# Layer-norm powers moved from GpSimd's power operation to a logarithm, an exponential and one Newton step, with a rewritten order table

## The reference

```python
def _ln_t(v, eps=1e-05):
    m = jnp.mean(v, axis=-1, keepdims=True)
    s = jnp.var(v, axis=-1, keepdims=True)
    return (v - m) / jnp.sqrt(s + eps)
...
t = t + _L1_attn_ref(_ln_t(t), ...)
t = t + _L1_ffn_ref(_ln_t(t), ...)
```

## Time and profile before

| | before |
|---|---|
| median of 3 runs | 2406.02 us (2404.33 to 2406.26) |
| the profiled execution, time | 2404.97 us |
| its span, first to last instruction | 2403.2 us |
| busy PE, DVE, POOL, ACT | 2183.1, 2062.3, 1839.2, 1516.3 us |

### The profile page before, as it was taken

The page is one execution under the profiler, slowest core; times in us unless marked ns, Lnnn a source line. Parts: engine busy times, 40 slices in busy tenths (PEclk is TensorE's granted clock), DMA queues, the critical chain, the costliest instruction groups (busy, mean ns, idle before and its releaser), DMA issues.

```text
span 2403.2 us, 44296 instructions
## 1 busy us (share of the span) xinstructions
PE 2183.1 (91%) x15620; PEld 1098.5 (46%) x15620; DVE 2062.3 (86%) x2694; ACT 1516.3 (63%) x2757; POOL 1839.2 (77%) x1553
## 2 busy tenths in 40 slices
PE   5379999999999999999999999999999999999972
PEld 5224444444444444444444444444444444444441
DVE  5257899999999999999999999999999999999853
ACT  0157767667666666666667666676676766766630
POOL 0314688888888888888888888888888888888786
PEclk8589999999999999999999999999999999999985
DMA  9442323323343243344432343344322333332111
GB/s 235 121 55 39 62 50 59 68 55 65 72 71 65 55 55 68 57 60 72 72 68 59 51 65 65 52 72 72 72 61 52 58 68 54 66 65 61 28 28 34
DMA packets 485705, 156.59 MB, mean 65 GB/s; under 512 B 438688, under 2 KB 472336, under 8 KB 485360
## 3 DMA queue, kind: packets, MB, share of 16 engines
q1 hardware_dynamic: 485488, 153.75, 35.1%
HBM read 95.41 MB, written 51.38 MB: 61 GB/s over the span
## 4 chain that ended last, share of the span: by engine, by line
POOL 35%; PE 25%; DVE 17%; ACT 10%; issue 10%; DMA 3%; SPq 0%; POOLq 0%; ACTq 0%; DVEq 0%
POOL rstd L819 11%; POOL qbuf L838 7%; DVE qbuf L1018 6%; POOL prod L877 5%; ACT ebuf L727 4%; PE ps L619 4%; POOL xn L825 4%; PE ps L645 3%; POOL prod L880 3%; PE ps L593 3%; PE ps L610 3%; PE ps L636 2%; ACT ebuf L722 2%; POOL xcs L833 2%; PE ps L658 2%
## 5 line engine op out<-in xcount | busy, mean ns | idle before, releaser
L727 ACT ACTIVATE ebuf<-ps,small 128x896 f32<-128x896 f32 x448 | 450.3, 1005 | 163.7 <-PE ps L610 150.0
L838 POOL TENSOR_TENSOR qbuf<-spread_r,qbuf 128x896 f32<-128x896 f32 x224 | 469.4, 2096 | 94.4 <-ACT spread_r L759 94.4
L1018 DVE SCALAR_TENSOR_TENSOR qbuf<-ps,ebuf 128x896 f32<-128x896 f32 x448 | 484.9, 1082 | 58.9 <-ACT ebuf L727 58.3
L1012 DVE SCALAR_TENSOR_TENSOR kbuf<-ps,ebuf 128x1024 f32<-128x1024 f32 (+1 forms) x416 | 487.6, 1172 | 48.2 <-ACT ebuf L722 44.7
L722 ACT ACTIVATE ebuf<-ps,small 128x1024 f32<-128x1024 f32 (+1 forms) x416 | 448.0, 1077 | 116.0 <-DVE kbuf L1012 68.2
L593 PE MATMUL ps<-kbuf,xcs 128*64 128x512 f32 (+1 forms) x1600 | 440.4, 611 | 7.7 <-DVE kbuf L1012 4.0
L819 POOL TENSOR_TENSOR rstd<-varr,power 112x28 f32<-112x28 f32 x64 | 307.2, 4800 | 164.9 <-DVE varr L996 164.8
L645 PE MATMUL ps<-qbuf,gmat 128*64 128x224 f32 x3584 | 386.2, 357 | 1.6 <-DVE pbuf L1041 1.0
L645 PEld LDWEIGHTS ps<-qbuf,gmat 128*64 128x64 f32 x3584 | 248.5, 136 | 154.6 <-issue 51.3
L1097 DVE TENSOR_TENSOR prod<-ps,gate 112x1024 f32<-112x1024 f32 x224 | 273.0, 1220 | 52.2 <-PE ps L670 37.1
L877 POOL TENSOR_TENSOR prod<-prod 112x512 f32<-112x512 f32 x224 | 285.6, 1275 | 20.9 <-DVE prod L1097 20.3
(11 more groups left out here) (132 smaller groups left out, 3129.0 us busy)
## 6 DMA issues: line engine op xcount, KB each, us to landing
z<-zd SPq DMA_DIRECT2D x256, 196.0 KB, 3.8
zd<-zhl SPq DMA_DIRECT2D x64, 392.0 KB, 2.4
qbuf<-in_x SPq DMA_DIRECT2D x16, 784.0 KB, 9.5
xt<-in_x SPq DMA_DIRECT2D x256, 49.0 KB
xd<-xn SPq DMA_DIRECT2D x128, 98.0 KB, 2.9
out<-ffn SPq DMA_DIRECT2D x256, 49.0 KB
xkt<-xd SPq DMA_DIRECT2D x32, 384.0 KB, 6.6
shifted<-nat SPq DMA_DIRECT2D x128, 52.6 KB, 5.3
```

The lines of the kernel that those rows point to most:

```text
L727: act.activation(ebuf[:, 1, 0:2 * G * PT].rearrange("p (a b) -> p a b", a=2), o[:, :, 0:G * PT], ACT.Exp, bias=minus_one).then_inc(qexp_ma ...
L838: nc.gpsimd.tensor_tensor(qbuf[:, 2:4, n, :], spread_r[:, :, :], qbuf[:, 2:4, n, :], ALU.mult)\
L1012: v.scalar_tensor_tensor(kbuf[0:w, m.at(KS, n) % 2, 0:DH * c].rearrange("p (a b) -> p a b", a=c), o[0:w, 0:c, :], 1.0, ebuf[0:w, 0, 0:DH * ...
L1018: v.scalar_tensor_tensor(qbuf[:, k0:k0 + 2, j, :], o[:, :, 0:G * PT], 1.0, ebuf[:, 1, 0:2 * G * PT].rearrange("p (a b) -> p a b", a=2), AL ...
```

## The change

The power of the two layer norms is taken apart. Before, POOL raised `varr` to -0.5 in one instruction. Now ACT takes a logarithm of the scaled variance, an exponential of -0.5 times that (a seed for the reciprocal root) and a square, as new steps LV1 and LV2 in ACT's order, each instruction waiting for the one ahead of it; POOL then makes one Newton step of three small instructions, again each waiting for the last. ACT's table of functions is named ahead of the loop, before ACT's first wait. Two other powers, ahead of the loop, stay.

```diff
+SEED = 2.0 ** -20
...
         @block.scalar
         def _(act):
+            nc.scalar.preload_act_table_set("natural_log_exp_and_others")
             act.wait_ge(dve_pre, 6)
...
+                elif kind in ("LV1", "LV2"):
+                    ln = kind == "LV2"
+                    act.wait_ge(var_made[ln], m.at(1, 1))
+                    act.activation(lnv[ln][:, :], varr[ln][:, :], ACT.Ln, scale=SEED * SEED).then_inc(seed_step[ln], 1)
+                    act.wait_ge(seed_step[ln], m.at(2, 1))
+                    act.activation(seed[ln][:, :], lnv[ln][:, :], ACT.Exp, scale=-0.5).then_inc(seed_step[ln], 1)
+                    act.wait_ge(seed_step[ln], m.at(2, 2))
+                    act.activation(newton[ln][:, :], seed[ln][:, :], ACT.Square, scale=SEED).then_inc(seed_made[ln], 1)
...
                 if kind in ("PN1", "PN2"):
                     ln = kind == "PN2"
-                    pool.wait_ge(var_made[ln], m.at(1, 1))
-                    nc.gpsimd.tensor_tensor(rstd[ln][:, :], varr[ln][:, :], power[0:PT, 0:SLOTS], ALU.pow)\
+                    pool.wait_ge(seed_made[ln], m.at(1, 1))
+                    nc.gpsimd.tensor_tensor(newton[ln][:, :], newton[ln][:, :], varr[ln][:, :], ALU.mult)\
+                        .then_inc(newton_step[ln], 1)
+                    pool.wait_ge(newton_step[ln], m.at(2, 1))
+                    nc.gpsimd.tensor_scalar(newton[ln][:, :], newton[ln][:, :], -0.5 * SEED, 1.5 * SEED, ALU.mult, ALU.add)\
+                        .then_inc(newton_step[ln], 1)
+                    pool.wait_ge(newton_step[ln], m.at(2, 2))
+                    nc.gpsimd.tensor_tensor(rstd[ln][:, :], seed[ln][:, :], newton[ln][:, :], ALU.mult)\
                         .then_inc(rstd_made[ln], 1)
```

All numbers of ORDER are new. Two lines of it, PE's F:

```diff
-        "F": [34.99, 35.66, 36.49, 37.53, 38.78, 40.49, 41.98],
+        "F": [37.013, 37.217, 38.036, 38.813, 40.476, 42.242, 43.704],
```

More of the change, by code:

```diff
@@ L122 @@
     "tensor": {
[17 rows of a table removed]
[17 rows of a table added]
     },
     "vector": {
[16 rows of a table removed]
[16 rows of a table added]
     },
     "scalar": {
[L160 to L176, removed]
+        "RP": [12.450, 13.105, 14.041, 16.732, 20.375, 21.053, 22.099],
+        "LV2": [28.369],
+        "Q": [1.811, 3.893, 4.483, 5.752, 6.814, 7.534, 8.276, 9.161, 9.621, 10.255, 11.173, 11.744, 13.631, 14.390],
+        "K": [-4.220, -2.668, -1.961, -1.175, -0.630, 0.549, 2.010, 2.988, 3.555, 4.162, 4.682, 5.312, 6.041],
@@ L177 @@
+        "XT": [-27.310, -21.925],
+        "XC": [-12.969],
+        "ZU": [30.311, 30.567],
+        "LV1": [-11.062],
+        "SU": [11.090, 17.319],
+        "RC": [11.593, 18.133],
+        "ZT": [-8.820, -6.627],
+        "RH": [11.944, 19.591],
+        "LG": [34.071],
+        "T2": [20.694, 23.115, 23.565, 26.340],
+        "KT": [7.734],
+        "RT": [36.319],
+        "S2": [22.515, 24.494, 25.702, 27.870],
+        "G": [8.621, 8.848],
+        "TB": [12.630],
     },
     "gpsimd": {
-        "F": [42.27, 43.77, 43.78, 45.54, 46.63, 48.87, 49.45],
@@ L180 @@
[L180 to L188, removed]
+        "PN2": [28.368],
+        "CS": [-2.821, 1.620],
+        "RP": [12.653, 13.588, 16.012, 19.574, 20.578, 21.256, 22.302],
+        "PN1": [-11.063],
+        "F": [37.426, 38.046, 38.652, 39.989, 41.168, 46.429, 46.930],
@@ L189 @@
+        "RL": [11.685, 19.350],
+        "OUT": [48.090],
+        "RF": [34.477, 35.843],
+        "T2": [21.918, 23.221, 23.886, 26.450],
+        "GT": [36.777],
     },
     "sync": {
[L191 to L196, removed]
+        "ZU": [30.810],
+        "CS": [-9.714, -5.162],
+        "OUT": [48.534],
+        "ZT": [-6.421],
+        "CV": [-18.952],
+        "XT": [-32.265],
@@ L295, in build @@
         varr = [sb(f"varr{k}", [PT, SLOTS]) for k in (1, 2)]
+        lnv = [sb(f"lnv{k}", [PT, SLOTS]) for k in (1, 2)]
+        seed = [sb(f"seed{k}", [PT, SLOTS]) for k in (1, 2)]
+        newton = [sb(f"newton{k}", [PT, SLOTS]) for k in (1, 2)]
         rstd = [sb(f"rstd{k}", [PT, SLOTS]) for k in (1, 2)]
@@ L397, in build @@
         recip_made = sem("recip_made")
+        seed_step = [sem(f"seed_step{k}") for k in (1, 2)]
+        seed_made = [sem(f"seed_made{k}") for k in (1, 2)]
+        newton_step = [sem(f"newton_step{k}") for k in (1, 2)]
         rhigh_made = sem("rhigh_made")
```

## The result

The changed kernel takes 2438.93 us in the median of 4 runs (2437.19 to 2443.62), the kernel before 2406.14 us beside it (4 runs, 2404.33 to 2407.95).

A forecast was written before the change was run, and what follows sets the result against it. PE, busy 65.86 of 68.28 us a period, was taken to bound the kernel. 28 periods at +1.55 us give +43.4, neighbouring periods +1, head and tail -8.3: +36, forecast 2442 us, 8-in-10 range 2415 to 2465.

The forecast's parts named there:

- rival in which POOL sets the period: POOL's power sets the period, so PE's idle time goes, at most 2.42 us a period: 2330 us; chance 0.07.
- Both stalls: Swapped neighbours make PE wait for DVE ahead of ZU0 (+1.0 us a period) and up to RP1 (+0.85); chance 0.71.
- rival with a single stall: Only ZU0's wait (+0.7 a period, 2417 us) or only RP1's (+0.55, 2413 us) is real; chance 0.13.
- Q0 ahead of F6: Swap on PE: ZU0 stands still until DVE has read Q0, 1.1 us less 0.1 regained behind: +1.0 a period.
- NM6 and CV0: NM6 behind K1 on DVE delays T2's last step 0.5 us; with CV0 ahead of F4 on PE, RP1 +0.85.
- R4: PE's 0.32 us idle ahead of R4, caused by POOL's late subtraction, goes with the power: -0.3 us a period.
- The sum of a period: One period changes by +1.0 + 0.85 - 0.3 = +1.55 us, over 28 periods +43.4 us.
- The other swaps: CV1/S22 and SM1/ZU1 on DVE, K12/LG and Q6/RT0 on ACT: readers come later; K12 may eat 0.1 or 0.2.
- LV1 and LV2 at no cost: New ACT work ahead of K7's and Q13's exponentials costs nothing, DVE being later; uncovered, up to 0.75 us a period.
- Ahead of and behind the periods: Outside the periods: table load at the start -1.3, first norm -3.1, last norm -3.9, together -8.3 us.
- The 1.39 us: PE's wait ahead of the second T2 step, ended by DVE's NM5 product behind PE's transpose ZT1, stays unchanged.
- rival with reloads: The set lacks a needed function and ACT reloads its table twice a norm: 164 us, up to 2600; chance 0.01.

## Why the prediction was right, point by point

**The order table, not the power, sets the time.** Shown: old power and new order give the same period as both together. The rival in which POOL sets the period falls with it: with the new power and the old order a period is only 0.20 to 0.48 us shorter, not 2.42.

**Both stalls are real.** With either place undone the kernel is still slower than the one before (2427.96 and 2414.57 us), so the rival with a single stall falls too.

**Q0 ahead of F6, predicted +1.0.** The wait is as predicted (1.00, ended by DVE's Q0, ZU0 one step later), and from XC to ZU0 PE takes 7.64 us in place of 6.61. But behind it 0.36 come back (ZU1 to SU1 3.05 for 3.41), where the prediction allowed 0.1. So the term was 0.67. The runs agree: Q0's swap undone gave 0.44, and SM1's another 0.23 (ZU1 to SU1 3.64, then 3.41). While ZU0 is late, the swap of SM1 and ZU1 costs nothing.

**NM6 and CV0, predicted +0.85.** It is 0.90, with the waits at the predicted places (0.53 and 0.51). The inner steps were less good. NM6's lateness alone costs 0.26, not 0.5, as PE has slack behind it. CV0 alone costs 0.55, not 0.7, and waits for ACT's copy of T2 as predicted. That the two errors leave the pair almost untouched is luck.

**R4, predicted -0.3.** In the old order the new power does what the prediction said, and more: 0.49 from LG to the first T2 step (5.23 to 4.74). In the new order K12 takes 0.22 of it, and -0.27 is left. But there the -0.27 does not need the power. With POOL's power and the new order the stretch is 4.96 us too, and PE waits for LG's copy only:

```profile
627.66 1.56 PE L664 MATMUL ps<-we,z 128*112 128x8 f16 x28
...
631.85 0.93 PE L636 MATMUL ps<-rs,sel 128*128 128x448 f16 x4 [0.16 <-ACT route L783]
632.62 0.39 PE L656 MATMUL ps<-eye_mean,t1b 128*112 128x132 f32 x2
```

POOL's subtraction (L850) begins at 627.57 in that kernel, 0.09 us ahead of LG; in the kernel before it begins at 619.87, 0.77 behind LG. The prediction gave this term to the power; in the changed kernel the order alone gives it, so that its size is nearly right is luck.

**The sum of a period.** +0.67 + 0.90 + 0.22 - 0.49 = +1.30, measured 1.32, predicted 1.55. Times 28 the period came out 6.6 us below the forecast: ZU0's term gives -9.2 of that (28 x 0.33), the others some 2.6 in the other direction. At the rim it was +1.76 for +1. The mechanism of the two stalls was right; that the total is so close owes something to errors of opposite sign.

**"The other swaps move steps whose readers come later."** This sentence failed for SM1 and ZU1, though it cost nothing as long as ZU0 waits; it was half right for K12.

**LV1 and LV2 at no cost.** Right in the periods of the changed kernel (69.60 us with them, 69.61 without), but for LV1 by luck: SM1 stands earlier there, which the prediction did not count. In the old order LV1 costs 0.28 us. It also costs once ahead of the periods of the changed kernel, where DVE is late with the variance and PE's next key step waits 2.68 us behind it (the exponentials of keys on either side begin 4.30 us apart, in the kernel before 2.50):

```profile
140.55 0.23 ACT L759 ACTIVATE lnv<-varr 112x28 f32<-112x28 f32 x1 [2.50 <-DVE varr L1020]
```

**Ahead of and behind the periods, predicted -8.3.** The tail is -3.65, predicted -3.9; the table load lies at the start now. The head is -2.76, predicted -4.4, and that number is soft: across the kernels with the new power the chain's first group of 24 DN matmuls lies between 164.47 and 175.13 us, so a single profile does not settle it. Against 36 us predicted for the profiled execution, 32.2 are the -6.6 of the periods and +2.7 from head, tail and rim.

**The 1.39 us, predicted unchanged.** They are, but not for the reason given, the work behind PE's ZT1: they go when NM5 is moved ahead of RT5.

**The table set.** By the Trainium skill, "ScalarE: Activation LUTs" (Table sets: the hidden batching unit), the named set holds logarithm and exponential; the trace agrees, with one load of 1283 ns in the whole program. The rival with reloads is out.

## What to carry to other kernels

When a code change comes with a new order, cost them apart: here the power was worth -0.48 us a period in the old order, once its wait stood in the right place of ACT's queue, and nothing in the new one, where a few neighbours in the order table cost 1.79. A new instruction that is short and "free" on an idle engine still holds back everything behind it until its input comes, so put it behind the work whose input is already there. And a stall taken away shows the next one: count on winning only a part of it (0.44 of 1.03 ahead of ZU0, 0.54 of 1.46 ahead of the second T2 step) unless the slack behind it is known.

## What was not expected of the hardware

**Three idle brackets on PE were smaller than the time that was won without the wait.** The 0.32 ahead of R4 were worth 0.49, the 0.53 ahead of T2's last step 0.70 up to that step, the 1.39 ahead of the second T2 step 1.46. PE's rows overlap: one of 0.55 us is followed by the next after some 0.38, so a wait of up to 0.17 can show no bracket. (The profile models the ends of PE's rows; how much of the overlap is the engine's own, no run here shows.) Slack is better read from the distance of two starts.

**A small DVE instruction that lasts until POOL's ends.** L1110 works on 112x28 and took 1.30 us (ended at 633.87, POOL's product at 633.83) and 0.70 us where it started later (625.16 to 625.86, POOL's product 623.72 to 625.82), but 0.17 us (from 628.57) where POOL's product had ended 0.34 us before (626.13 + 2.10 = 628.23). In the changed kernel it took 1.17 us and ended 0.04 behind the product again. The Trainium skill, "SBUF — State Buffer" (SBUF: two separate sides), says that some DVE instructions and those of GpSimd share a pair of ports as an exclusive lock, for the whole instruction. The rows agree; the instructions beside it that read PSUM went on beside POOL's product at their usual 0.38 and 1.08 us.
